# Attention and mixture of experts on one core: norms of batches 0 and 1 ahead of the down weights' low parts, their transposes in the last slot, statistics of batch 2 later

## What is computed

```
def reference(x, ctx_1024, ...):
    x = x + xattn(layernorm(x), ctx_1024, ctx_1024, Wq, bq, Wk, bk, Wv, bv, Wo, bo)   # causal, 16 heads
    x = x + ffn(layernorm(x), gate_w, w_up, w_down, sg_gate, sg_up, sg_down)
    return x

def ffn(x, ...):
    logits = x @ gate_w.T
    topk_logits, topk_idx = top_k(logits, 2)
    ...                                  # softmax of the two
    for e in range(8):
        out = out + comb[:, e:e+1] * ((silu(x @ wg[e].T) * (x @ wu[e].T)) @ w_down[e].T)
    shared = (silu(x @ sg_gate.T) * (x @ sg_up.T)) @ sg_down.T
    return shared + out
```

## Time and profile before

| | us |
|---|---|
| median of 3 runs | 490.18 |
| lowest and highest | 489.74, 491.91 |
| profiled execution, device time | 491.95 |
| its span | 490.2 |
| TensorE busy in the span | 456.6 (93%) |
| VectorE busy | 315.1 (64%) |
| ScalarE busy | 218.9 (45%) |
| GpSimd busy | 212.3 (43%) |

### The profile page before, as it was taken

How to read it: one execution, slowest core, us unless ns; L and a number is a source line. 1 busy time by engine, 2 the same in 40 slices (tenths; PEclk the granted TensorE clock), 3 DMA queues, 4 the chain that set the end, 5 groups by cost and what they waited for, 6 DMA issues and landing times.

```text
span 490.2 us, 10348 instructions
## 1 busy us (share of the span) xinstructions
PE 456.6 (93%) x3257; PEld 328.0 (67%) x3258; DVE 315.1 (64%) x651; ACT 218.9 (45%) x429; POOL 212.3 (43%) x212
## 2 busy tenths in 40 slices
PE   7989989899999999989978999999999999999993
PEld 6764444664548454655565546699999999999852
DVE  4975767577663857666965896855555555554446
ACT  2257676727572566566854343332332233223210
POOL 4115676734540436302712003136676676665420
PEclk9989999999999999998999999999999999999998
DMA  8593422422224121400498801014444434444379
GB/s 274 100 226 97 131 72 72 147 64 70 75 77 151 37 93 54 142 21 2 124 379 327 304 0 43 7 38 72 68 65 68 77 71 65 68 73 66 36 207 337
DMA packets 45580, 53.93 MB, mean 110 GB/s; under 512 B 7760, under 2 KB 41872, under 8 KB 44912
## 3 DMA queue, kind: packets, MB, share of 16 engines
q1 hardware_dynamic: 34320, 39.77, 25.2%
q0 software_dynamic: 7488, 10.31, 12.9%
q10 hardware_dynamic: 3744, 3.47, 2.7%
HBM read 27.09 MB, written 13.67 MB: 83 GB/s over the span
## 4 chain that ended last, share of the span: by engine, by line
PE 60%; DVE 17%; ACT 7%; DMA 6%; issue 4%; SPq 3%; ACTq 0%; DVEq 0%; POOLq 0%
PE set_a L989 6%; PE set_a L659 6%; PE set_a L990 6%; PE set_a L988 6%; PE set_b L689 5%; ACT attention L1139 3%; DVE attention L1385 3%; PE set_b L1007 3%; PE set_a L896 3%; PE set_b L679 3%; PE set_b L1008 3%; PE set_b L1009 3%; ACT attention L1060 3%; PE set_b L998 3%; PE set_a L701 2%
## 5 line engine op out<-in xcount | busy, mean ns | idle before, releaser
L1385 DVE TENSOR_REDUCE attention<-set_a 128x2 f32<-128x1024 f32 (+2 forms) x96 | 96.0, 1042 | 25.0 <-PE set_a L661 23.0
L1139 ACT ACTIVATE attention<-set_b 128x512 f32<-128x512 f32 (+1 forms) x176 | 87.9, 568 | 48.3 <-PE set_b L679 35.0
L543 POOL TENSOR_SCALAR_AFFINE_SELECT attention<-attention 128x512 f32<-128x512 f32 x64 | 42.5, 679 | 89.3 <-ACT attention L1139 89.3
L623 POOL DMA_INDIRECT sum_rows<-moe,token_of x39 | 61.8, 1585 | 44.0 <-issue 29.0
L659 PE MATMUL set_a<-attention 96*128 96x512 bf16 (+3 forms) x256 | 62.2, 308 | 5.1 <-DVE attention L1385 4.8
L1252 ACT ACTIVATE moe<-set_a 128x384 f32<-128x384 f32 x39 | 19.2, 492 | 105.1 <-PE set_a L990 105.1
L615 POOL DMA_INDIRECT e_x<-normed_rows,token_of x39 | 39.4, 1010 | 61.3 <-DVE token_of L1584 34.9
L679 PE MATMUL set_b<-attention 99*128 99x512 bf16 (+3 forms) x256 | 59.7, 307 | 3.4 <-ACT attention L1139 1.1
L1609 DVE TENSOR_TENSOR moe<-set_a,moe 128x384 f32<-128x384 f32 x39 | 21.8, 558 | 62.9 <-ACT moe L1252 62.9
L659 PEld LDWEIGHTS set_a<-attention 96*128 96x128 bf16 x256 | 25.6, 100 | 45.1 <-DVE attention L1385 22.4
L988 PE MATMUL set_a<-wup_hi,e_xT_hi 128*128 x156 | 53.0, 340 | 0.0
(11 more groups left out here) (179 smaller groups left out, 897.3 us busy)
## 6 DMA issues: line engine op xcount, KB each, us to landing
attention<-attention SPq DMA_DIRECT2D x182, 64.0 KB, 2.6
wup<-in_wupT SPq DMA_DIRECT2D x2, 3072.0 KB, 14.8
sum_rows<-attention SPq DMA_DIRECT2D x2, 2048.0 KB, 13.3
wup<-sum_rows SPq DMA_DIRECT2D x8, 512.0 KB, 7.0
attention<-in_ctxT SPq DMA_DIRECT2D x7, 512.0 KB, 5.5
w_down<-in_wdnT SPq DMA_DIRECT2D x3, 1024.0 KB, 5.2
x_res<-in_x SPq DMA_DIRECT2D x4, 512.0 KB, 6.4
out<-x_res ACTq DMA_DIRECT2D x8, 256.0 KB, 4.1
```

The source lines that it names most:

```text
L623: g.indirect_dma_start(acc[i], bass.IndirectOffsetOnAxis(token_of[:, t:t + 1], 0), e_y[:, t % 2, :], None, compute_op=ALU.add).then_inc(ad ...
L1139: nc.scalar.activation(pT[k][:, h:h + heads, :], bank(par)[:, 0:heads * (S - k * P)], ACT.Exp).then_inc(b_free, 1)
L1385: v.tensor_reduce(dst, src, AX.X, ALU.max, negate=True).then_inc(a_free, 1)
```

## The change

VectorE's statistics of batch 2 move from the end of batch 2 to behind the first maxima of the last batch. The variances of batches 0 and 1 are made at the end of batch 2, their square root between ScalarE's second and third high part. In the last batch VectorE norms batches 0 and 1 directly after its last maxima and copies their transposes itself; TensorE makes these in the last slot, in the banks that the maxima used, where fillers stood. Two low parts, the variances of batch 2, a third low part and the norm of batch 2 follow, then the division; three low parts come behind that. The moments of batches 0 to 2 thus fall into two steps, and batch 3's are numbered 4. Batch 2 is now written out for VectorE, for its last part differs. The diff, cut to its core:

```
-        LAST = [("PV", 0), ("PV", 1), ("BUSY", 14), ("S", 0), ("S", 1), ("S", 2)]
-        for j, turns in ((3, 4), (4, 5), (5, 4), (6, 4), (7, 4)):
-            LAST += [("BUSY", turns), ("S", j)]
+        LAST = [("PV", 0), ("PV", 1), ("LN", 0), ("LN", 1), ("LN", 2), ("LN", 3), ("S", 0), ("S", 1), ("S", 2)]
+        for j in range(3, 7):
+            LAST += [("LN", j + 1), ("S", j)]
+        LAST += [("BUSY", 4), ("S", 7)]
...
+            def ln2_early(step):
+                b, part = divmod(step, 4)
+                if part == 0:
+                    pe.wait_ge(xs_ready, B + b + 1)
+                    pe.wait_ge(a_free, A_PRO + (B - 1) * A_PER + 2 * A_GRP)
+                for i in range(2):
+                    c, j = divmod(2 * part + i, QT)
+                    last = tr(A[:, 2 * b + c, j * P:(j + 1) * P], xn2[:, b * QT + j, c * P:(c + 1) * P], ident[:])
+                if part == 3:
+                    last.then_inc(l2_full, 1)
...
-                    ln2_transposes(0)
-                    n_b, par_b = n_b + C, par_b + C
+                    pe.wait_ge(l2_free, 2)
...
-                    ln2_transposes(1)
+                    ln2_transposes(2)
...
-                if final:
-                    ln2_transposes(2)
-                else:
+                if not final:
...
                     for i in range(2 * M):
+                        if i == 2:
+                            deviations(2, 0, 2 * QT)
                         down_hi(i)
...
-                    deviations(2, 0, T - QT)
+                    deviations(3, 2 * QT, 3 * QT)
                     p_v(NG - 1, count + NG - 1)
-                    ln2_copies(0)
-                    ln2_copies(1)
+                    ln2_copies(2)
...
+            def ln2_copy(b):
+                dve.wait_ge(l2_full, b + 1)
+                v.tensor_copy(xn2T[:, :, b * S:(b + 1) * S], pair(A, b)).then_inc(l2_free, 1)
...
+                    if final and g == 1:
+                        dve.wait_ge(a_free, A_PRO + b * A_PER)
+                        row_stats(b - 1)
                 if final:
-                    for i in range(2 * M):
-                        down_lo(i)
-                    moments(2, 0, T - QT, 2 * T - QT)
+                    reciprocals(2, 0, 2 * QT)
                     normalised(0, ln2_row(0)).then_inc(xs_ready, 1)
                     normalised(1, ln2_row(1)).then_inc(xs_ready, 1)
+                    ln2_copy(0)
+                    ln2_copy(1)
+                    down_lo(0)
+                    down_lo(1)
+                    variances(3, 2 * QT, 3 * QT, 2 * T - QT)
+                    down_lo(2)
+                    reciprocals(3, 2 * QT, 3 * QT)
+                    normalised(2, ln2_row(2)).then_inc(xs_ready, 1)
...
                 if final:
-                    normalised(2, ln2_row(2)).then_inc(xs_ready, 1)
+                    for i in range(3, 2 * M):
+                        down_lo(i)
+                if before_last:
+                    variances(2, 0, 2 * QT, T + 2 * QT)
```

More of the change, by code:

```diff
@@ L262, in build @@
         mean_done = sem("mean_done")
+        l2_full, l2_free = sem("l2_full"), sem("l2_free")
         in_high, in_low = sem("in_high"), sem("in_low")
@@ L349, in build @@
         B_LAST = B_ATT + B * B_PER - B_SLOT - 1 - NA
-        B_LN2 = [B_LAST, B_LAST + C, B_LAST + 2 * C + NA, B_LAST + 3 * C + NA]
+        B_LN2 = {2: B_LAST, 3: B_LAST + C + NA}
         assert B == 4
@@ L784, in slot @@
                     elif kind == "BUSY":
-                        busy(pv_bank[:, 0:P] if order is FIRST else A[:, 3, 0:P], j)
+                        if order is LAST:
+                            pe.wait_ge(l2_free, 1)
+                        busy(pv_bank[:, 0:P] if order is FIRST else A[:, 1, 0:P], j)
+                    elif kind == "LN":
+                        ln2_early(j)
                     elif kind == "MAX" and rows:
@@ L808, in logits @@
                     pe.wait_ge(ld_moe, DMA * 4)
-                pe.wait_ge(b_free, B_LN2[b] + C)
+                if b in B_LN2:
+                    pe.wait_ge(b_free, B_LN2[b] + C)
+                else:
+                    pe.wait_ge(l2_free, b + 1)
                 dst = pv_bank[:, b * P:(b + 1) * P] if b < B - 1 else A[:, 3, 0:P]
@@ L1177, in batch @@
                 if final:
-                    deviations(2, 0, T - QT)
+                    deviations(3, 2 * QT, 3 * QT)
                     p_v(NG - 1, count + NG - 1)
-                    ln2_copies(0)
-                    ln2_copies(1)
-                    n, par = n + 2 * C, par + 2 * C
+                    ln2_copies(2)
+                    n, par = n + C, par + C
                 else:
@@ L1206, in logits_copy @@
                 copy(lgT[:, cols], src).then_inc(lt_read, 1)
-            ln2_copies(2)
             logits_copy(0, slice(0, S - P), pv_bank[:, 0:S - P])
-            deviations(3, T - QT, T)
+            deviations(4, T - QT, T)
             gate = [A[:, 0, :], A[:, 2, :]]
@@ L1294, in _, with variances @@
             v = nc.vector
-            def moments(i, lo, hi, seen):
+            def variances(i, lo, hi, seen):
                 me, mo, qe, qo = (stats[:, lo:hi, k] for k in (1, 4, 2, 5))
@@ L1313, in moments, with reciprocals @@
                 v.tensor_tensor(a, a, c, ALU.add).then_inc(ln_step, 1)
+            def moments(i, lo, hi, seen):
+                variances(i, lo, hi, seen)
+                reciprocals(i, lo, hi)
+            def reciprocals(i, lo, hi):
                 dve.wait_ge(std_ready, i + 1)
@@ L1408, in down_lo, with row_stats, batch @@
                                 ALU.subtract).then_inc(dn_lo, 1)
-            def batch(b, final):
+            def row_stats(b):
+                for j in range(QT):
+                    v.bn_stats(stats[:, bass.ds(b * QT + j, 1), :],
+                               xs_all[:, bass.ds(b * QT + j, 1), :]).then_inc(st_done, 1)
+            def ln2_copy(b):
+                dve.wait_ge(l2_full, b + 1)
+                v.tensor_copy(xn2T[:, :, b * S:(b + 1) * S], pair(A, b)).then_inc(l2_free, 1)
+            def batch(b, final, before_last=False):
                 n, par = A_PRO + b * A_PER, A_PRO
@@ L1449, in batch @@
                                 ALU.add).then_inc(a_free, 1)
-                dve.wait_ge(a_free, n + 1)
-                for j in range(QT):
-                    v.bn_stats(stats[:, bass.ds(b * QT + j, 1), :],
-                               xs_all[:, bass.ds(b * QT + j, 1), :]).then_inc(st_done, 1)
+                if not before_last:
+                    dve.wait_ge(a_free, n + 1)
+                    row_stats(b)
             def ln2_row(b):
                 return lambda j: xn2[:, b * QT + j:b * QT + j + 1, 0:D]
-            with dve.Fori(0, B - 1) as b:
+            with dve.Fori(0, B - 2) as b:
                 batch(b, False)
+            batch(B - 2, False, True)
             batch(B - 1, True)
-            moments(3, T - QT, T, 2 * T)
+            moments(4, T - QT, T, 2 * T)
             normalised(3, ln2_row(3)).then_inc(xs_ready, 1)
```

## The result

The changed kernel took 488.32 us in the median of 17 runs (486.55 to 490.73), the kernel before 491.40 in 17 runs beside them (489.74 to 492.82): a ratio of 0.9946 with an interval of 0.9931 to 0.9960.

The account below looks back on a forecast made before the run. VectorE's instruction order was taken as the bound from the end of batch 2 through the last batch. Gains of 2.1 + 1.75 + 0.55 = 4.4 us from the median 490.18 gave 485.8 us, range 484.2 to 489.0.

Parts of the forecast that it names:

- the Sum: Whole kernel: gains of 2.1, 1.75 and 0.55 make 4.4 us, taken from the median 490.18 to give 485.8.
- Part 1: Entry of the last batch: statistics move into a VectorE wait, so maxima begin earlier; gain 2.1 us, bounds 0 to 3.0.
- The analog: Entry: as in batch 2, the row of maxima is written 9.39 us after the first maximum's start, at 224.9.
- The tables: Entry, ScalarE: two added table loads and a square root make 2.8 us; first exponential at 218.8, before 219.12.
- The margin: Entry: ScalarE would write the row of maxima at 224.55, no later than the 224.9 from batch 2's analog.
- Part 2: VectorE at the end: reordered work readies the attention rows at 251.8 instead of 253.54; gain 1.75 us, between 0.2 and 2.0.
- Rival (b): VectorE at the end: slow low parts beside GpSimd make part 2 nothing or -0.4, 487.5 to 487.9 us; chance 0.13.
- Part 3: TensorE's order: batch 2's transposes go ahead of the attention's, projection 1.9 us behind the rows instead of 2.44; gain 0.55.
- Covers: End: three leftover low parts (3.6 us) cost nothing behind the normalisation, inside VectorE's 4.64 us wait for the projection.
- Downstream: After the last residual's sum: every wait moves along with the gain, so none of the 4.4 us is given back.
- Rival (c): End: TensorE falls to 1.2 GHz while waiting for VectorE, 7.6 us more, 493.4 us; chance 0.06.

Follow-up runs that it names:

- e1: The kernel before, run again unchanged for a second trace; 491.68 us, ratio 1.0011.
- e7: The changed kernel with the first two low parts before and between VectorE's two copies instead of behind them; 489.39 us, ratio 0.9938.
- f2: The changed kernel with idle products at the start (26 to 28 us) and between the router's transposes; 488.59 us, ratio 0.9948.
- f5: The changed kernel with idle products at the start, in the last batch's three waits and between the router's transposes; 487.25 us, ratio 0.9935.
- e5: The changed kernel with filler matmuls in TensorE's three waits between the last probabilities and the projection; 486.92 us, ratio 0.9916.
- e10: The changed kernel, unchanged, for a third trace; 489.04 us, ratio 0.9957.
- e11: The changed kernel, unchanged, for a fourth trace; 489.05 us, ratio 0.9943.
- e8: The kernel before with filler matmuls at 26 to 28 us, ahead of the program's first row maxima; 492.11 us, ratio 1.0013.
- e6: The changed kernel with filler matmuls at 26 to 28 us, ahead of the program's first row maxima; 486.88 us, ratio 0.9913.
- f4: The changed kernel with idle products between the router's transposes alone; 486.68 us, ratio 0.9921.

## Why the prediction was right or wrong

**The sum against the measurement.** 485.8 was forecast and 488.32 measured, 2.5 us more: 0.75 because the sum was 4.4 in place of 3.65; 1.22 because it was taken from a median of 490.18, of three runs, where the kernel before has 491.40 in seventeen; and 0.57 because the medians show 3.08 of the 3.65.

Two steps of the prediction failed: the size of part 1, explained below, and the level from which the Sum subtracts, 490.18. By the groups of runs 490.18 is the level of the kernel before without a fall (490.45 in 54 runs); 3.65 below it lies 486.5, and the changed kernel's executions in that group took 487.00. The median execution of either kernel has a fall, and the Sum has no term for that. That 488.32 still lies in the range is in part luck: its upper end was made for parts that come out smaller, and what filled it was mostly the level.

**Part 1 (2.1 predicted, 1.39 measured, and 0.19 of batch 2).** This is the step of the mechanism that failed, a term that was too large. The analog was right about the new order: 9.39 was carried over from batch 2, 9.08 came out. What was wrong is what it was subtracted from, 227.06 - 217.0 = 10.06, which held the fall of the clock; in e1 the same step takes 8.92. The sentence "the analog of batch 2 assumes that this goes with the wait" named the weak point and didn't price the other case: the gain is then just the moved 1.41 us of statistics. The bounds (0 to 3.0) held it. So the same fall was counted twice: the execution's 1.77 above the median was taken off, and its lost time was booked as gain as well.

**The tables.** The margin was judged rightly. Counted from the start of the residual's sum, the first exponential begins at 4.69 (predicted 4.5) and the row is written at 10.22 (predicted 10.25 by ScalarE, 10.6 by the analog). The Trainium skill, ScalarE: Activation LUTs, section "What ACT_TABLE_LOAD costs", gives a drain of about 1.38 us with each switch; the rows show 1.28 for the load and 0.01 to 0.03 on either side of it, so here the trace decides against the drain.

**Part 2 (1.75 predicted).** From the end of the last maxima to the attention's rows 17.2 was worked out, and it is 17.19 (231.23 to 248.42), before 18.96: gain 1.77. The terms erred against each other: the eight norms took 3.14 in place of 2.67, and the variances 1.7 in place of 1.05, but the three low parts 4.0 in place of 4.5, so that the sum is this close is partly luck. The copies took 1.22 and 1.23, as guessed. Rival (b) did not come, for no low part on the path met a long GpSimd addition; e7 shows that such a meeting does happen (3.40), there partly inside a wait.

**Part 3 (0.55 predicted, 0.3 measured).** The projection starts 1.93 behind the rows, as predicted (1.9). Before it was 2.28 by the timeline, which shows the first product at 255.82; the 255.98 of the earlier trace rows gave 2.44. From its start to the sum it takes 3.73, before 3.65. In all the end gains 2.08, predicted 2.3.

**Covers.** The three low parts left over ended at 251.83, inside the projection and not ahead of it as the prediction had it, but 2.26 before VectorE was needed. Downstream all moved along.

**Rival (c)** was given 0.06 as a fixed effect. It is neither absent nor fixed: f2 lost 1.69 of the 7.6 by it, the changed kernel's own four traces nothing. That falls behind the new waits are what keeps the changed kernel's executions so seldom free of them (9 of 45 against 54 of 133) is possible, but not shown. For it: f2's trace, and the good medians of f5 and e5, which fill these waits. Against: f2's is the only fall there in eleven traces; e10 and e11 fall at 262 to 270 and 28 to 34, places where traces of the kernel before (e8, with the start filled, for the first) fall too, and e6 and f4 have good medians without filling the new waits. What sets the place stays open.

## What to carry to other kernels

Before a difference from one trace goes into a sum, look at the granted clock in that stretch and price the term once with the fall and once without; a moved step is worth its own length unless an undisturbed trace shows more. Size a reordering by a stretch between two landmarks in two traces of the same kernel, which repeated to 0.07 us here while medians of six to seventeen runs moved by 1. Subtract from a baseline whose number of runs is like that of the result's.

## What the runs showed of the hardware that was not expected

- One program shows its falls to 1.2 GHz at different places in different executions: the kernel before at 28 to 34 and 220 to 224 us, the changed kernel at 28 to 34 and 262 to 270, versions of them also at 66 to 74, 250 to 256 and 266 to 272. In e1 TensorE waited 1.5 us for VectorE ahead of one; in f2 the waits ahead of it were 0.98, 0.89 and 0.78. The same waits came without a fall in other executions. Three were priced: 1.16 us in the entry (12.42 against 11.26), 1.23 in the router (33.70 against 32.47) and 1.69 in the projection.
- Instructions of VectorE on four columns took 0.15 us in most places, and 0.59 and 0.60 twice at 242 us, while GpSimd was masking; the variances lost some 0.9 us by that.
